# A two-layer transformer decoder: the first layer's inverse roots taken by VectorE from the variance's bits, in place of ScalarE's logarithm and exponential

## The chip, the cores and the metric

The kernel runs on one core of a Trainium2 chip. Its time is the device time of one execution in microseconds (us). The median of three runs before the change is 869.42 us (866.59 to 870.5). The engines are called PE (TensorE), DVE (VectorE), ACT (ScalarE), POOL (GpSimd) and SP (SyncE, which here only issues transfers) in the rows of the profile.

## The reference, cut to what matters

The input `x` is 16 sequences of 128 tokens with 128 numbers each. Layer 0 is self attention, cross attention and a mixture of experts, layer 1 is attention, a cosine block and a quantised MLP. Each step reads the normalised `x` and adds its result to `x`:

```python
def _layernorm(x, axis=-1, eps=1e-05):
    m = jnp.mean(x, axis=axis, keepdims=True)
    v = jnp.var(x, axis=axis, keepdims=True)
    return (x - m) / jnp.sqrt(v + eps)

x = x + _L0_attn_ref(_layernorm(x, axis=-1), ...)    # 16 heads of 8 numbers, causal
x = x + _L0_xattn_ref(_layernorm(x, axis=-1), ctx_768, ...)
x = x + _L0_ffn_ref(_layernorm(x, axis=-1), ...)
```

The change concerns `1 / sqrt(v + eps)` of the first two of these normalisations, 2 x 16 tiles of 128 tokens. The inverse roots are numbers of one per token: 128 partitions x 1 for a tile, and 128 x 4 for the four tiles of a group that are treated together.

## The kernel before, in words

`layer0_attentions` runs both attentions of layer 0 as one pipeline over N = 32 steps: t = 0 to 15 is the self attention of sequence t, t = 16 to 31 the cross attention of sequence t - 16. The loop is unrolled, from t = -4 to 32, and each engine has its own list of instructions in this order; only semaphores tie them together. In iteration t:

- PE computes the scores of step t (`scores`, lines 454 and 458: the second needs a row of maxima that SP's transfer has laid out), transposes the maxima of t + 1 and projects the output of t - 1 (`back_part`), makes queries and keys of t + 3 and transposes the normalised tile of t + 4, in cross attention the context tile `l_cb` too (`front_part`, line 407), multiplies with the floors (line 467, cross attention), computes the raw scores of t + 2 for the row maxima (`maxima`, line 442) and multiplies probabilities with values (`values`, line 485).
- DVE: reciprocal of the sums of t - 1 (`finish`, line 704), a copy (`expand_values`), the normalised output (`weighted`), the normalised tile of t + 4 (`normalise`, while that tile belongs to the first sixteen), the clips in cross attention (line 699), the statistics of the new `x` (line 658), and four reductions for the maxima of t + 2 (`top`, line 684), with `moments` between the first and the second of them and other small work between the second and the third. PE's `scores(t + 1)` waits for all four reductions of `top` (semaphore `maxed`).
- ACT: four exponentials of step t (line 545), copies of PE's results (lines 558 and 525), and the split of the queries for t + 3 (line 539, in cross attention 533 and 536).
- POOL: adds the output bias (line 335), adds the attention's result to `x` (line 358), splits the keys (line 340), and normalises the tiles of the cross attention (line 330).

The inverse roots are made for four tiles at a time. k = 0 is the input's normalisation, group g = 0 to 3 of the sixteen input tiles; k = 1 is the normalisation ahead of cross attention, for the tiles that self attention has finished. DVE adds eps (`variance`). ACT takes the logarithm and then the exponential of -0.5 times it (`roots`, lines 579 and 581; each of the two is preceded by a load of an activation table). DVE improves the result by one Newton step of three instructions (`scales`, lines 649, 651, 653), y(1.5 - 0.5 v y^2).

Their places: `roots(0, 0)` and `scales(0, 0)` ahead of the loop; `roots(0, g)` at the end of t = -2, 2, 6 and `scales(0, g)` at t = -1, 3, 7, behind `normalise` and ahead of the statistics; `variance(1, g)` at t = 4, 8, 12, 16 between the second and the third reduction of `top`; `roots(1, g)` at the end of t = 5, 9, 13, 17; `scales(1, g)` at t = 6, 10, 14, 18 between the second and the third reduction.

Ahead of everything ACT issues nine transfers, the last seven of them the self attention's weights (semaphore `weights`, which PE and DVE wait for as a whole), the last being `self_bo`. At t = 3 SP issues the cross attention's weights, in 22 transfers, and from t = 2 on it writes a blank pattern to memory for the expert stage.

## Time and profile before

| | |
|---|---|
| median of three runs | 869.42 us |
| the profiled execution's own time | 870.21 us |
| its span (first to last instruction) | 867.4 us |
| PE busy | 623.3 us (72%), 6449 matmuls |
| DVE busy | 532.8 us (61%), 1414 instructions |
| ACT busy | 379.7 us (44%), 884 instructions |
| POOL busy | 217.1 us (25%), 312 instructions |
| layer 0's two attentions | from 0 to about 300 us |

The page gives busy time and instructions of each engine, and the groups of instructions that cost most. Busy shares are means over stages with different limits. The attention stage is read best from a timeline, which lists instructions in the order of their start with their duration, and in brackets how long the engine was idle before them and what ended that. "issue" there means that nothing in the profile shows what the engine waited for. Reading one engine's timeline from a line to the same line of the next iteration gives the length of an iteration.

### The profile page before, as it was taken

Reading aid. Unit: us, or ns where it says so; the run is one execution under the profiler, and the core shown is the slowest. Engines: PE = TensorE matmul, PEld = TensorE weight load, DVE = VectorE, ACT = ScalarE, POOL = GpSimd, SP = SyncE. Lnnn points to the kernel's source line nnn. Section 1 sums busy time; section 2 is a strip of 40 time slices with the busy share of each in tenths; the row PEclk is TensorE's granted clock in tenths of the full one; section 3 lists DMA queues with packets and bytes.
Section 4 is the critical chain, followed back from the end, with each engine's and each line's share of the span. In section 5 each row is a group of like instructions: output and inputs, shape, how many; then the busy total and the mean of one; then the engine's idle time right before and its main releaser. Section 6 shows DMA issues by size and latency. Waiting matters only on the chain. (4 is left out here: it accounts for less than half of the span.)

```text
span 867.4 us, 17861 instructions
## 1 busy us (share of the span) xinstructions
PE 623.3 (72%) x6449; PEld 460.8 (53%) x6449; DVE 532.8 (61%) x1414; ACT 379.7 (44%) x884; POOL 217.1 (25%) x312
## 2 busy tenths in 40 slices
PE   3896999889999572056665714989999973875765
PEld 1453555556666362045655602667787852653554
DVE  3463565587788563236564467565665733877995
ACT  6464656777666321033333302543525334543332
POOL 3132223344342116513232214132221310000000
PEclk9798999999999955579999965999999995556797
DMA  3013153341110031155555530000000001000000
GB/s 91 2 43 95 53 127 102 102 104 36 52 27 8 5 140 48 44 195 226 223 212 219 216 98 0 2 2 2 2 2 2 2 1 28 14 1 0 12 13 24
DMA packets 54146, 55.81 MB, mean 64 GB/s; under 512 B 10492, under 2 KB 44862, under 8 KB 54062
## 3 DMA queue, kind: packets, MB, share of 16 engines
q1 hardware_dynamic: 50493, 49.52, 17.7%
q0 software_dynamic: 2272, 4.27, 1.5%
q8 instruction: 51, 0.84, 0.4%
q10 hardware_dynamic: 1296, 0.92, 0.4%
q14 instruction: 34, 0.27, 0.1%
HBM read 16.66 MB, written 14.49 MB: 36 GB/s over the span
## 5 line engine op out<-in xcount | busy, mean ns | idle before, releaser
L545 ACT ACTIVATE l_probs<-bank 128x512 f32<-128x512 f32 x128 | 66.1, 603 | 98.0 <-PE bank L458 97.9
L1073 ACT ACTIVATE experts_h<-bank,experts_wb 128x128 f32<-128x128 f32 x156 | 44.5, 368 | 86.0 <-PE bank L1047 81.7
L1432 POOL COPY ptx<-over_pt 32x512 f32<-32x512 f32 x64 | 38.9, 607 | 128.1 <-DVE over_pt L1402 120.3
L1080 POOL DMA_INDIRECT results<-experts_y,experts_dest x39 | 40.2, 1030 | 99.8 <-DVE experts_y L1115 99.3
L1040 PE MATMUL bank<-ident,experts_xb 128*128 128x128 f32 x39 | 13.2, 338 | 67.4 <-DMA experts_xb<-slots 67.4
L699 DVE SCALAR_TENSOR_TENSOR l_probs<-l_probs,bank 128x512 f32<-128x512 f32 x64 | 41.1, 684 | 24.9 <-PE bank L467 23.1
L684 DVE TENSOR_REDUCE l_m<-bank 128x4 f32<-128x512 f32 x64 | 40.9, 678 | 19.4 <-PE bank L442 19.4
L454 PE MATMUL bank<-l_qxx,l_front 32*128 32x512 f32 x256 | 37.4, 651 | 19.2 <-issue 15.5
L358 POOL TENSOR_TENSOR x<-x,l_back 128x128 f32<-128x128 f32 x32 | 14.5, 454 | 132.5 <-ACT l_back L558 121.4
L1040 PEld LDWEIGHTS bank<-ident,experts_xb 128*128 128x128 f32 x39 | 5.5, 142 | 74.7 <-DMA experts_xb<-slots 74.7
L1332 ACT ACTIVATE ke<-bank 64x512 f32<-64x512 f32 x64 | 37.9, 592 | 16.3 <-PE bank L1263 15.5
L1047 PE MATMUL bank<-experts_xt,experts_wb 128*128 128x128 f32 x312 | 43.1, 283 | 0.0
L658 DVE BATCH_NORM_STATS2 l_stats<-x 128x6 f32<-128x128 f32 x32 | 9.3, 291 | 54.3 <-POOL x L358 54.3
L1055 PE MATMUL bank<-experts_wb,experts_h 128*128 128x128 f32 x312 | 41.3, 275 | 0.3 <-ACT experts_h L1073 0.3
L684 DVE TENSOR_REDUCE l_m_raw<-bank 128x4 f32<-128x512 f32 x64 | 40.7, 673 | 0.0
L1047 PEld LDWEIGHTS bank<-experts_xt,experts_wb 128*128 128x128 f32 x312 | 39.5, 198 | 0.0
L892 POOL DMA_INDIRECT slots<-xs,route_pos x32 | 30.9, 966 | 29.6 <-DVE route_pos L964 20.4
L1055 PEld LDWEIGHTS bank<-experts_wb,experts_h 128*128 128x128 f32 x312 | 38.0, 192 | 0.5 <-ACT experts_h L1073 0.5
L1306 PE MATMUL bank<-over_ot,over_wo 128*128 128x128 f32 x256 | 33.3, 284 | 6.0 <-DVE over_ot L1408 6.0
L1375 DVE COPY over_q<-bank 128x512 f32<-128x512 f32 x32 | 22.1, 690 | 24.7 <-PE bank L1263 24.7
L1099 DVE COPY experts_xt<-bank 128x128 f32<-128x128 f32 x39 | 11.4, 291 | 41.0 <-PE bank L1040 40.9
L340 POOL TENSOR_TENSOR l_kxx<-l_front,heads 128x512 f32<-128x512 f32 x32 | 33.3, 1039 | 11.9 <-ACT l_front L525 10.6
(318 smaller groups left out, 1709.1 us busy)
## 6 DMA issues: line engine op xcount, KB each, us to landing
experts_wb<-w SPq DMA_DIRECT2D x39, 578.0 KB
slots<-blank SPq DMA_DIRECT2D x16, 528.0 KB, 4.7
w<-in_w SPq DMA_DIRECT2D x16, 256.0 KB
experts_xb<-slots SPq DMA_DIRECT2D x39, 66.0 KB, 1.8
experts_both<-results SPq DMA_DIRECT2D x8, 256.0 KB, 5.1
x<-in_x SPq DMA_DIRECT2D x4, 256.0 KB, 3.9
out<-x SPq DMA_DIRECT2D x4, 256.0 KB, 2.3
l_cb<-in_ctx SPq DMA_DIRECT2D x16, 48.0 KB
```

Of the source, the lines that this page charges most:

```text
L340: nc.gpsimd.tensor_tensor(kxx[t % 2][:, :, :], front[(t - 3) % 4][:, 1, :].rearrange("p (a k) -> p a k", a=1).broadcast_to([128, 4, S]), M ...
L454: nc.tensor.matmul(score_bank[g][:, :], k[r, :], qxx[t % 4][r, :, :].rearrange("p j q -> p (j q)"), start=True, stop=False, skip_group_che ...
L545: nc.scalar.activation(probs[t % 2][:, g, :], score_bank[g][:, :], ACT.Exp, scale=SCALE0).then_inc(s["probs"], 1)
L684: nc.vector.tensor_reduce(mx[:, 4 * g:4 * g + 4], top_bank[g][:, :].rearrange("p (j k) -> p j k", j=4), AX.X, ALU.max, negate=True).then_i ...
L699: nc.vector.scalar_tensor_tensor(probs[t % 2][:, g, :], probs[t % 2][:, g, :], 1.0, floor_bank[g][:, :], ALU.min, ALU.max).then_inc(s["cli ...
L1047: mm = nc.tensor.matmul(up_bank[j % 2][:, c * S:(c + 1) * S], wb[j % 4][:, W1 + c * 128:W1 + (c + 1) * 128], xt[j % 2][:, :], start=True, ...
L1055: mm = nc.tensor.matmul(down_bank[j % 2][:, 0:D], h[j % 2][:, c, :], wb[j % 4][:, W2 + c * D:W2 + (c + 1) * D], start=(c == 0), stop=(c == 3))
L1073: nc.scalar.activation(h[j % 2][:, c, :], up_bank[j % 2][:, c * S:(c + 1) * S], ACT.Gelu_apprx_tanh, bias=wb[j % 4][:, B1 + c:B1 + c + 1]) ...
L1080: nc.gpsimd.indirect_dma_start(M.results, bass.IndirectOffsetOnAxis(dest[j % 4][:, 0:1], 0), y[j % 4][:, :], None, bounds_check=2 * B * S ...
L1306: mm = nc.tensor.matmul(y_bank[:, 0:S], wo[:, r, :], ot[t % 2][:, r, :], start=r == 0, stop=r == PAIR - 1)
L1332: nc.scalar.activation(ke[h, r, j, :], ring[at_block(t, r, 1) % 3][h, :], ACT.Copy).then_inc(s["ke"], 1)
L1432: nc.gpsimd.tensor_copy(ptx[t % 2][r, :, r], pt[t % 2][r, :, :]).then_inc(s["spread"], 1)
```

## The change

`roots` and ACT's part in it are gone. DVE makes a first estimate from the variance's bits: it shifts the pattern right by one and subtracts it from the constant 0x5F3759DF, both on 32-bit integers, and then takes three Newton steps of the same three instructions as before. That is SCALE_STEPS = 11 instructions in place of three, each of which waits for the one before it. They are cut in three parts: the estimate and the first Newton step (five instructions), the second step (three), the third (three). For k = 0 the parts stand at t = -3, -2, -1 (group 1), 1, 2, 3 (group 2) and 5, 6, 7 (group 3), at the place where `scales` stood; for k = 1 at t = 4, 5, 6 (group 0), 8, 9, 10, then 12, 13, 14, then 16, 17, 18, between the second and the third reduction. Group 0 of the input is done in one piece ahead of the loop.

```diff
-                def roots(k, g):
-                    r = slice(B * k + 4 * g, B * k + 4 * g + 4)
-                    wait(act, s[f"var{k}"], g, plus=1)
-                    nc.scalar.activation(log[:, r], var[:, r], ACT.Ln).then_inc(s[f"ln{k}"], 1)
-                    wait(act, s[f"ln{k}"], g, plus=1)
-                    nc.scalar.activation(root[:, r], log[:, r], ACT.Exp, scale=-0.5).then_inc(s[f"root{k}"], 1)
...
-                roots(0, 0)
...
-                    if t in (-2, 2, 6):
-                        roots(0, (t + 6) // 4)
-                    if t in (5, 9, 13, 17):
-                        roots(1, (t - 5) // 4)
...
+GUESS, SCALE_STEPS = float(0x5F3759DF), 11
+PARTS = range(0, 5), range(5, 8), range(8, SCALE_STEPS)
...
-                def scales(k, g):
+                def scales(k, g, steps):
...
+                    for n in steps:
+                        if n == 0:
+                            wait(dve, s[f"var{k}"], g, plus=1)
+                            V.tensor_scalar(half[k][:, :], var[:, r].bitcast(I32), 1, None, ALU.logical_shift_right).then_inc(s[f"newton{k}"], 1)
+                            continue
+                        wait(dve, s[f"newton{k}"], g, per=SCALE_STEPS - 1, plus=n)
+                        if n == 1:
+                            V.tensor_scalar(root[:, r].bitcast(I32), half[k][:, :], -1.0, GUESS, ALU.mult, ALU.add).then_inc(s[f"newton{k}"], 1)
+                        elif n % 3 == 2:
+                            V.scalar_tensor_tensor(square[k][:, :], root[:, r], -0.5, root[:, r], ALU.mult, ALU.mult).then_inc(s[f"newton{k}"], 1)
+                        elif n % 3 == 0:
+                            V.tensor_tensor(slope[k][:, :], square[k][:, :], var[:, r], ALU.mult).then_inc(s[f"newton{k}"], 1)
+                        elif n < SCALE_STEPS - 1:
+                            V.scalar_tensor_tensor(root[:, r], slope[k][:, :], 1.5, root[:, r], ALU.add, ALU.mult).then_inc(s[f"newton{k}"], 1)
+                        else:
+                            V.scalar_tensor_tensor(rstd[:, r], slope[k][:, :], 1.5, root[:, r], ALU.add, ALU.mult).then_inc(s[f"ready{k}"], 1)
...
-                scales(0, 0)
+                scales(0, 0, range(SCALE_STEPS))
...
-                    if t in (-1, 3, 7):
-                        scales(0, (t + 5) // 4)
+                    if t in (-3, -2, -1, 1, 2, 3, 5, 6, 7):
+                        scales(0, (t + 7) // 4, PARTS[(t + 3) % 4])
...
-                    if t in (6, 10, 14, 18):
-                        scales(1, (t - 6) // 4)
+                    if 4 <= t < 19 and t % 4 != 3:
+                        scales(1, t // 4 - 1, PARTS[t % 4])
```

At the start, on ACT, this stood between the weights' transfers and the first copy of a front in the program before:

```order
L593 ACT_TABLE_LOAD
L593 ACTIVATE self_identb<-ident 128x128
L579 ACT_TABLE_LOAD
L579 ACTIVATE l_log<-l_var 128x4
L581 ACT_TABLE_LOAD
L581 ACTIVATE l_root<-l_log 128x4
L525 ACTIVATE l_front<-bank 128x128
```

and this stands there after the change (the lines are numbered anew):

```order
L588 ACT_TABLE_LOAD
L588 ACTIVATE self_identb<-ident 128x128
L529 ACTIVATE l_front<-bank 128x128
```

The logarithm and the exponential are gone with their two table loads. In the rest of ACT's attention stage no load is left; the next one is that of the routing's square root.

On DVE, iteration t = 8, this stood between the statistics of the finished tile and the reciprocal of the next iteration in the program before:

```order
L658 BN_STATS l_stats<-x 128x6
L684 TENSOR_REDUCE l_m<-bank 128x4
L663 BN_AGGR l_mv<-l_stats 128x2
L684 TENSOR_REDUCE l_m<-bank 128x4
L642 TENSOR_SCALAR l_var<-l_mv 128x4
L684 TENSOR_REDUCE l_m<-bank 128x4 x2
L704 RECIPROCAL l_rden<-bank 128x128
```

and this after the change:

```order
L659 BN_STATS l_stats<-x 128x6
L685 TENSOR_REDUCE l_m<-bank 128x4
L664 BN_AGGR l_mv<-l_stats 128x2
L685 TENSOR_REDUCE l_m<-bank 128x4
L632 TENSOR_SCALAR l_var<-l_mv 128x4
L642 TENSOR_SCALAR l_half<-l_var 128x4
L646 TENSOR_SCALAR l_root<-l_half 128x4
L648 SCALAR_TENSOR_TENSOR l_square<-l_root 128x4
L650 TENSOR_TENSOR l_slope<-l_square,l_var 128x4
L652 SCALAR_TENSOR_TENSOR l_root<-l_slope,l_root 128x4
L685 TENSOR_REDUCE l_m<-bank 128x4 x2
L705 RECIPROCAL l_rden<-bank 128x128
```

The five instructions of part 0 have come between the variance and the third reduction. At t = 9 nothing stood there before, and part 1 stands there now:

```order
L659 BN_STATS l_stats<-x 128x6
L685 TENSOR_REDUCE l_m<-bank 128x4
L664 BN_AGGR l_mv<-l_stats 128x2
L685 TENSOR_REDUCE l_m<-bank 128x4
L648 SCALAR_TENSOR_TENSOR l_square<-l_root 128x4
L650 TENSOR_TENSOR l_slope<-l_square,l_var 128x4
L652 SCALAR_TENSOR_TENSOR l_root<-l_slope,l_root 128x4
L685 TENSOR_REDUCE l_m<-bank 128x4 x2
L705 RECIPROCAL l_rden<-bank 128x128
```

Here the three reductions behind `moments`, which followed each other, are cut in one and two. At t = 10 the same three names stand in the same place before and after.

## Rows read from the trace of the kernel before

**Rows 1.** The page, part 1: busy us (share) x instructions of TensorE.
```profile
PE 623.3 (72%) x6449; PEld 460.8 (53%) x6449; DVE 532.8 (61%) x1414; ACT 379.7 (44%) x884; POOL 217.1 (25%) x312
```

**Rows 2.** Line 579 alone: count, ns min/median/max, first and last start.
```profile
L579 ACT ACT_TABLE_LOAD  x8: 1283/1283/1283, 7.2 to 184.1; - x8
```

**Rows 3.** Timeline, ScalarE: start, duration, instruction, [idle before it, releaser].
```profile
117.34 1.28 ACT L579 ACT_TABLE_LOAD   x1
...
121.12 2.06 ACT L545 ACTIVATE l_probs<-bank 128x512 f32<-128x512 f32 x4 [0.76 <-PE bank L458]
...
187.03 2.04 ACT L545 ACTIVATE l_probs<-bank 128x512 f32<-128x512 f32 x4
```

**Rows 4.** Timeline, VectorE, iterations t = 9 and 10.
```profile
111.43 0.95 DVE L704 RECIPROCAL l_rden<-bank 128x128 f32<-128x128 f32 x1
...
119.26 0.95 DVE L704 RECIPROCAL l_rden<-bank 128x128 f32<-128x128 f32 x1
...
125.91 0.16 DVE L649 SCALAR_TENSOR_TENSOR l_square<-l_root 128x4 f32<-128x4 f32 x1
126.10 0.16 DVE L651 TENSOR_TENSOR l_slope<-l_square,l_var 128x4 f32<-128x4 f32 x1
...
127.57 0.95 DVE L704 RECIPROCAL l_rden<-bank 128x128 f32<-128x128 f32 x1
```

**Rows 5.** Timeline, TensorE, the scores of t = 10 and 11.
```profile
119.45 1.14 PE L454 MATMUL bank<-l_qxx,l_front 32*128 32x512 f32 x8 [0.43 <-issue]
...
127.75 1.14 PE L454 MATMUL bank<-l_qxx,l_front 32*128 32x512 f32 x8 [0.90 <-issue]
```

**Rows 6.** Timeline, TensorE, the iterations t = 18 and 19.
```profile
184.75 1.14 PE L454 MATMUL bank<-l_qxx,l_front 32*128 32x512 f32 x8 [0.44 <-issue]
...
188.80 0.33 PE L407 MATMUL bank<-ident,l_cb 128*128 128x128 f32 x1 [0.43 <-DMA l_cb<-in_ctx]
...
193.98 1.14 PE L454 MATMUL bank<-l_qxx,l_front 32*128 32x512 f32 x8 [0.98 <-issue]
...
197.43 0.27 PE L407 MATMUL bank<-ident,l_cb 128*128 128x128 f32 x1
```

**Rows 7.** Timeline, start: VectorE, TensorE; then `self_bo`: issue, us to landing.
```profile
10.22 0.16 DVE L649 SCALAR_TENSOR_TENSOR l_square<-l_root 128x4 f32<-128x4 f32 x1 [4.66 <-ACT l_root L581]
11.08 0.22 DVE L161 COPY self_wq<-self_wide_q 128x128 f32<-128x128 f32 x1
14.16 0.29 DVE L675 COPY v_exp<-bank 128x128 f32<-128x128 f32 x1 [0.75 <-PE bank L475]
...
11.31 0.45 PE L404 MATMUL bank<-ident,l_xn 128*128 128x128 f32 x1 [11.31 <-DVE l_xn L668]
...
4.93 0.59 ACTq L151 DMA_DIRECT2D self_bo<-in_self_bo  x1
...
DMA to landing us min/median/max: 5.7/5.7/5.7
```

**Rows 8.** Timeline, VectorE, then GpSimd, at t = 12, 13 and 18.
```profile
142.29 0.42 DVE L642 TENSOR_SCALAR l_var<-l_mv 128x4 f32<-128x4 f32 x1
...
149.97 1.85 DVE L684 TENSOR_REDUCE l_m<-bank 128x4 f32<-128x512 f32 x3
...
192.13 0.15 DVE L649 SCALAR_TENSOR_TENSOR l_square<-l_root 128x4 f32<-128x4 f32 x1
...
142.22 0.46 POOL L335 TENSOR_TENSOR x<-x,cross_bo 128x128 f32<-128x128 f32 x1
...
150.46 0.46 POOL L335 TENSOR_TENSOR x<-x,cross_bo 128x128 f32<-128x128 f32 x1
...
191.97 0.82 POOL L330 TENSOR_SCALAR l_xn<-x,l_mv,l_rstd 128x128 f32<-128x128 f32 x1
```

**Rows 9.** Timeline, VectorE, t = 1.
```profile
43.57 0.29 DVE L658 BATCH_NORM_STATS2 l_stats<-x 128x6 f32<-128x128 f32 x1 [1.67 <-POOL x L358]
```

**Rows 10.** Timeline, TensorE, t = 5.
```profile
79.39 2.07 PE L458 MATMUL bank<-row,self_side 128*128 128x512 f32 x4 [7.89 <-DMA row<-l_back]
```

More of the change, by code:

```diff
@@ L209, in layer0_attentions @@
         s = semaphores(nc, "l0", """x0 x1 x2 x3 consts weights prepared masks heads cleared floors
-            stats0 aggr0 stats1 aggr1 var0 ln0 root0 square0 slope0 ready0 var1 ln1 root1 square1 slope1 ready1 xn cload front_ps front qd qxx kxx v_exp
+            stats0 aggr0 stats1 aggr1 var0 newton0 ready0 var1 newton1 ready1 xn cload front_ps front qd qxx kxx v_exp
             smax_ps maxed m_clip back_ps back mt_hi mt row st_ps probs pv rden o_norm x_done
@@ L231, in layer0_attentions @@
         mv, rstd = sb("mv", [S, N, 2]), sb("rstd", [S, N])
-        var, log, root = sb("var", [S, N]), sb("log", [S, N]), sb("root", [S, N])
+        var, root = sb("var", [S, N]), sb("root", [S, N])
+        half = [sb(f"half{k}", [S, 4], I32) for k in range(2)]
         square, slope = [sb(f"square{k}", [S, 4]) for k in range(2)], [sb(f"slope{k}", [S, 4]) for k in range(2)]
@@ L642, in variance @@
                     nc.vector.tensor_scalar(var[:, r], mv[:, r, 1], EPS_LN, None, ALU.add).then_inc(s[f"var{k}"], 1)
-                def scales(k, g):
+                def scales(k, g, steps):
                     r = slice(B * k + 4 * g, B * k + 4 * g + 4)
-                    wait(dve, s[f"root{k}"], g, plus=1)
-                    nc.vector.scalar_tensor_tensor(square[k][:, :], root[:, r], -0.5, root[:, r], ALU.mult, ALU.mult).then_inc(s[f"square{k}"], 1)
-                    wait(dve, s[f"square{k}"], g, plus=1)
-                    nc.vector.tensor_tensor(slope[k][:, :], square[k][:, :], var[:, r], ALU.mult).then_inc(s[f"slope{k}"], 1)
-                    wait(dve, s[f"slope{k}"], g, plus=1)
-                    nc.vector.scalar_tensor_tensor(rstd[:, r], slope[k][:, :], 1.5, root[:, r], ALU.add, ALU.mult).then_inc(s[f"ready{k}"], 1)
+                    V = nc.vector
+                    for n in steps:
[14 more added lines that the diff above has]
+                            V.scalar_tensor_tensor(rstd[:, r], slope[k][:, :], 1.5, root[:, r], ALU.add, ALU.mult).then_inc(s[f"ready{k}"], 1)
                 def statistics(t):
```

## The prediction, made before the changed kernel was run

> **What bounds the kernel now.** I read the page first: TensorE is busy 72% of the span [rows 1], and the change does not touch it, so the question is which waits of TensorE the touched engines end. I then looked for the stage that the change reaches, which is the first 195 us of 867.4, and read ScalarE, VectorE and TensorE there in order of time.
>
> ScalarE is what the change relieves. It loads an activation table 16 times for eight pairs of logarithm and exponential, 1283 ns each [rows 2]; line 581 has as many loads of the same length as the row of line 579 shows. But most of these pairs stand in idle time. The pair of t = 9 begins at 117.34 and is over before 121.12, and the first exponential of the next iteration still waits 0.76 us for TensorE [rows 3]. Only the pair of t = 17 makes it late: that exponential starts at 187.03, right behind the pair, with no wait in its row [rows 3].
>
> What sets the pace is a loop of two engines: TensorE's maxima feed four reductions on VectorE (`top`), and the next scores (line 454) wait for the last of these. The reader should see it in two numbers that agree. An iteration without small instructions among the reductions takes 119.26 - 111.43 = 7.83 us on VectorE; the one with three of them takes 127.57 - 119.26 = 8.31, which is 0.48 more [rows 4]. And TensorE's idle time before line 454 goes from 0.43 to 0.90 us at the same place, 0.47 more, though the row names "issue" there and not VectorE [rows 5]. So whatever stands between the second and the third reduction is paid in full.
>
> **What the change takes away.** ScalarE loses 16 x 1.283 = 20.5 us of table loads [rows 2] and 16 small activations. By the idle times above nearly nothing of it is on the path. At t = 17 the late exponential is hidden by something else: TensorE's line 407 waits until 188.80 for the transfer of `l_cb`, while in iteration t = 19 it starts 197.43 - 193.98 = 3.45 us after line 454, and here it would have started at 184.75 + 3.45 = 188.20 [rows 6]. This wait of 0.6 us is not ScalarE's, so I count nothing for the relief at t = 17.
>
> At the start VectorE waits 4.66 us for the first root, until 10.22, and three instructions later the first tile is normalised; TensorE begins at 11.31 [rows 7]. Now the eleven instructions start at 10.22 - 4.66 = 5.56 and take 11 x 0.2 = 2.2 us, so rstd is there at 7.8 instead of 10.8. That is 3.0 us, but what is late next is the weights: TensorE waits for all seven transfers, and the last one (`self_bo`) is issued at 4.93 and lands 5.7 us later, at 10.63 [rows 7]. I let TensorE begin at 10.70. Lower bound of the gain: VectorE's copy, which needs the same transfers, starts at 11.08, so they had landed by then, which leaves 0.2 us. Upper bound: 3.0 us, if the landing were early. I take 11.31 - 10.70 = 0.61, the landing's own row. Against it stands the next place: at t = -3 five new instructions come ahead of `expand_values`, where VectorE had 0.75 us idle [rows 7]; 5 x 0.19 = 0.95 us, so 0.20 is paid. The start brings 0.61 - 0.20 = **0.4 us**.
>
> **What the change adds.** The step from one dependent small instruction to the next is 126.10 - 125.91 = 0.19 us [rows 4], and I use it for the new ones, integer ones included (bounds: 0.15, the shortest duration among them, and 0.42, the longest [rows 8]).
>
> For the input's groups (t = -2 to 7) the parts follow `normalise`, and VectorE then waits for GpSimd. The shortest such wait is that of t = 1, behind the statistics of four tiles, 1.67 us [rows 9]; the five new instructions there take 0.95. Nothing of these parts is paid.
>
> For the second normalisation's groups the parts stand between the second and the third reduction, in three iterations of every four. Part 0 (five instructions, behind a variance that stands there already) costs 5 x 0.19 = 0.95; part 1 costs 0.47, as the three instructions do today; part 2 has three instructions where three stood, so nothing. Per place:
> - t = 4: part 0, 0.95. Hidden: TensorE waits 7.89 us for the row's transfer until 79.39 in the next iteration [rows 10], and that transfer is queued behind the cross weights on SP, not behind VectorE.
> - t = 5, 9: part 1, 0.47 each; t = 8, 12, 16: part 0, 0.95 each. Paid.
> - t = 13: part 1, 0.47. Here the second reduction and the two behind it start at 149.97 and take 1.85, so the first new instruction would start at about 150.56, while GpSimd's addition runs from 150.46 to 150.92 [rows 8]. Under the same addition, begun at 142.22, the variance at 142.29 took 0.42 us [rows 8] where such instructions take 0.16; so 0.26 more, 0.73.
> - t = 17: part 1, 0.47. Line 454 moves to 185.22, line 407 could start at 188.67, and `l_cb` lands at 188.80 as before [rows 6]: hidden. SP issues that transfer without asking VectorE.
>
> Sum: 2 x 0.47 + 3 x 0.95 + 0.73 = 4.5 us. All places together cost 4.5 + 0.95 + 0.47 = 5.9 if nothing hides.
>
> The 0.26 at t = 13 agrees with a rule of the Trainium skill, page "SBUF — State Buffer", section "SBUF: two separate sides": a VectorE instruction with two inputs in SBUF and a GpSimd instruction that reads SBUF lock each other out for the whole instruction. By the rule GpSimd's TENSOR_SCALAR (line 330) would lock too, and part 1 of t = 17 would wait some 0.5 us for it, of which the `l_cb` wait hides a little: the sum would be 0.4 us higher. The trace speaks against that: with line 330 running from 191.97 to 192.79, the SCALAR_TENSOR_TENSOR at 192.13 took its usual 0.15 us [rows 8]. I leave it out.
>
> **Sum.** -0.4 + 4.5 = +4.1 us. The profiled execution took 870.21 us around its span of 867.4; 4.1 more gives 874.3. It was 0.8 above the median of the runs, 869.42; from the median the forecast is **873.5 us**, 0.47% slower. What this kernel's measurement can tell from no change is about 0.5%, 4.35 us, so the forecast lies just inside "same".
>
> **Rivals.**
> 1. *No cover (slower).* The places t = 4 and t = 17 are paid as well, and the weights land at 11.0, so the start gives nothing. For it: the row transfer of t = 5 and `l_cb` may come earlier when VectorE's side is later. Against it: 7.89 us is a wide cover. The price is +5.9, 875.3. It decides as soon as one of both places is paid along with a start of under 0.2 us gain. Chance 13%.
> 2. *The integer pair is slow (slower).* The shift and the subtraction, at 0.42 us like the longest row instead of 0.16, cost 2 x 0.26 at each of t = 8, 12, 16: +1.6 on the forecast, 875.1. For it: no integer operation of this size stands in VectorE's rows. Against it: at four elements the kind of number should not matter. Chance 6%.
> 3. *The reductions are not what TensorE waits for (not slower).* If "issue" in the row of line 454 means its own sequencer, and the loop's extra 0.48 us at t = 10 came from elsewhere, the added instructions are free. What is left is the start, -0.4, and perhaps the 0.6 us of t = 17: 868.4 to 869.0. For it: the label. Against it: both views give the same 0.47. Chance 13%.
> 4. *The whole start is saved.* If TensorE can begin at 8.3, the start gives 3.0 - 0.2 = 2.8 us and the change costs 4.5 - 2.8 = +1.7, 871.1. Against it: the landing row. Chance 6%.
> 5. *ScalarE sets the pace (faster).* Then the 20.5 us of loads go from the path and 4.5 come back: 853.4. Against it: the 0.76 us idle behind the pair. Chance 2%.
>
> **How the numbers follow.** The forecast has 60%. Its own range is 871.7 to 875.3: the start between 0.2 and 0.9, each part's step between 0.15 and 0.22, and the scatter of the medians (the three runs before lie 3.9 us apart). The range that should hold the time 8 times in 10 takes in rivals 1, 2 and 4: 870.2 to 876.7. Slower by over 0.5% means above 873.8: 42% of the forecast's 60%, and most of rivals 1 and 2, together 41%. Faster by over 0.5% is rival 5 and a tail of rival 3, 4%. The rest is 55%.
>
> **What would show it.** In the profile after: TensorE's first matmul at about 10.7; no table load on ScalarE between the first one and the routing; VectorE's step from the reciprocal (the old line 704) to the next at t = 8, 12 and 16 longer by 0.95 than the variance alone made it, at t = 5, 9 and 13 by 0.47 to 0.73; line 454's idle time longer by as much; t = 4 and t = 17 without effect on the row's and `l_cb`'s waits, which get shorter instead. The first attention stage would end 4.1 us later, and the stages behind it take the same time as before. The prediction is wrong if line 454 keeps 0.43 us of idle at t = 9, or if the difference stands behind 300 us, where nothing was changed.

## The result, and the profile of the changed kernel

The changed kernel takes 875.55 us (median of six runs, 874.67 to 878.4) against 868.63 (864.99 to 870.5) for the kernel before on the same chip: the ratio is 1.0093, with a 95% interval of 1.0066 to 1.0119. Two later comparisons, described with the experiments, give 1.0057 and 1.007; all three together make the changed kernel 6.1 ± 1.0 us slower. So it is slower, by more than the bound of 0.5%; the forecast of 873.5 us was too low and its "same" wrong, though the time lies inside the range given.

The page's busy times answer to [rows 1]:

```profile
PE 615.1 (70%) x6419; PEld 458.1 (52%) x6449; DVE 543.8 (62%) x1478; ACT 356.2 (41%) x852; POOL 217.9 (25%) x312
```

ScalarE is busy 23.5 us less, VectorE 11.0 us more, and the span is 873.5 us instead of 867.4. The kernel became slower although the sum of busy time fell by more than it rose.

ScalarE's table loads answer to [rows 2]. These are all that the timeline of the changed kernel shows before 320 us (start, duration, instruction, idle time before it and what ended it):

```profile
5.17 1.28 ACT L588 ACT_TABLE_LOAD   x1 [5.17 <-issue]
...
309.88 1.28 ACT L195 ACT_TABLE_LOAD   x1 [2.69 <-PEq L119]
```

VectorE's timeline of the changed kernel, iterations t = 8 and 9, answers to [rows 4]:

```profile
104.38 0.94 DVE L705 RECIPROCAL l_rden<-bank 128x128 f32<-128x128 f32 x1
...
111.00 0.16 DVE L632 TENSOR_SCALAR l_var<-l_mv 128x4 f32<-128x4 f32 x1
111.20 0.17 DVE L642 TENSOR_SCALAR l_half<-l_var 128x4 int32<-128x4 int32 x1
111.40 0.17 DVE L646 TENSOR_SCALAR l_root<-l_half 128x4 int32<-128x4 int32 x1
111.61 0.16 DVE L648 SCALAR_TENSOR_TENSOR l_square<-l_root 128x4 f32<-128x4 f32 x1
111.80 0.16 DVE L650 TENSOR_TENSOR l_slope<-l_square,l_var 128x4 f32<-128x4 f32 x1
112.00 0.16 DVE L652 SCALAR_TENSOR_TENSOR l_root<-l_slope,l_root 128x4 f32<-128x4 f32 x1
...
113.28 0.94 DVE L705 RECIPROCAL l_rden<-bank 128x128 f32<-128x128 f32 x1
...
121.57 0.94 DVE L705 RECIPROCAL l_rden<-bank 128x128 f32<-128x128 f32 x1
```

The five new instructions begin 0.20 us apart, the integer ones too. From reciprocal to reciprocal, t = 8 takes 113.28 - 104.38 = 8.90 us and t = 9 takes 8.29.

TensorE's timeline of the changed kernel shows the scores that come out of it, and answers to [rows 5]:

```profile
104.56 1.14 PE L458 MATMUL bank<-l_qxx,l_front 32*128 32x512 f32 x8 [0.43 <-issue]
...
113.46 1.14 PE L458 MATMUL bank<-l_qxx,l_front 32*128 32x512 f32 x8 [1.51 <-issue]
...
121.75 1.14 PE L458 MATMUL bank<-l_qxx,l_front 32*128 32x512 f32 x8 [0.90 <-issue]
```

The idle time ahead of the scores grows from 0.43 to 1.51 us behind part 0 and to 0.90 behind part 1.

This gives a ruler for the whole stage: the step from one iteration's scores to the next (line 454 before, 458 after), in us. Each kernel of the experiments below was read with it (columns: iteration t; "copy" is a second profile of the kernel before; "1, 2, 3" are three profiles of the changed kernel):

```
 t    before   copy   | changed 1     2      3   | parts_out all_out before_out four_steps
 4      7.90   7.90   |    8.90    8.91   8.91   |   7.90     7.82     7.90       8.91
 5     17.24  19.47   |   16.75   16.62  18.51   |  18.89    18.26    17.31      18.68
 6      8.31   8.29   |    8.30    8.30   8.29   |   7.85     7.83     7.83       8.29
 7      7.81   7.83   |    7.82    7.83   7.82   |   7.82     7.83     7.84       8.30
 8      7.90   7.90   |    8.90    8.92   8.90   |   7.92     7.83     7.92       8.90
 9      7.83   7.82   |    8.29    8.30   8.32   |   7.83     7.82     7.82       8.29
12      8.25   8.25   |    9.33    9.33   9.33   |   8.07     8.01     8.26       9.34
13      7.94   7.94   |    8.65    8.66   8.65   |   7.95     7.95     7.93       8.65
16      9.43  10.04   |   10.41   10.96  10.64   |   9.52     9.66    10.00       9.91
17      8.10   8.10   |    8.60    8.60   8.60   |   8.11     8.12     8.12       8.60
18      9.23   9.37   |    8.78    9.30   9.30   |   9.31     9.13     8.97       8.96
```

Most rows repeat to 0.03 us between profiles of one kernel. Those with a transfer in them (t = 5, 16 and 18) scatter, and so does the first step (t = 0), which is about 9.1 us in some profiles and 10.2 to 10.6 in others. Two single steps outside this table stand out as well: t = 15 of parts_out (8.03 against 7.41) and t = 13 of second_only (10.01 against 8.65); both are taken up below.

At t = 12 and 13 one new instruction each time meets GpSimd's addition, as forecast for t = 13. VectorE's, then GpSimd's timeline of the changed kernel, which answer to [rows 8]:

```profile
144.86 0.41 DVE L642 TENSOR_SCALAR l_half<-l_var 128x4 int32<-128x4 int32 x1
...
153.92 0.40 DVE L648 SCALAR_TENSOR_TENSOR l_square<-l_root 128x4 f32<-128x4 f32 x1
...
188.48 0.16 DVE L648 SCALAR_TENSOR_TENSOR l_square<-l_root 128x4 f32<-128x4 f32 x1
...
144.79 0.45 POOL L339 TENSOR_TENSOR x<-x,cross_bo 128x128 f32<-128x128 f32 x1
...
153.84 0.46 POOL L339 TENSOR_TENSOR x<-x,cross_bo 128x128 f32<-128x128 f32 x1
...
188.37 0.79 POOL L334 TENSOR_SCALAR l_xn<-x,l_mv,l_rstd 128x128 f32<-128x128 f32 x1
```

The two small instructions that begin under line 339's addition take 0.41 and 0.40 us and end when it ends (144.86 + 0.41 = 145.27 against 144.79 + 0.45 = 145.24); the one under line 334's TENSOR_SCALAR takes 0.16. On this the rule of the Trainium skill that the prediction weighed ("SBUF — State Buffer", section "SBUF: two separate sides") and the trace differ again at the same place: by the rule line 334 would have locked too.

At the start, VectorE's, GpSimd's and TensorE's timelines of the changed kernel answer to [rows 7]:

```profile
7.85 0.16 DVE L654 SCALAR_TENSOR_TENSOR l_rstd<-l_slope,l_root 128x4 f32<-128x4 f32 x1
...
10.01 0.23 DVE L164 COPY self_wq<-self_wide_q 128x128 f32<-128x128 f32 x1 [1.62 <-DMA self_bo<-in_self_bo]
...
13.00 1.04 DVE L652 SCALAR_TENSOR_TENSOR l_root<-l_slope,l_root 128x4 f32<-128x4 f32 x1
...
13.97 0.28 DVE L676 COPY v_exp<-bank 128x128 f32<-128x128 f32 x1
...
12.99 1.04 POOL L344 TENSOR_TENSOR l_kxx<-l_front,heads 128x512 f32<-128x512 f32 x1 [1.49 <-ACT l_front L529]
...
10.07 0.45 PE L408 MATMUL bank<-ident,l_xn 128*128 128x128 f32 x1 [10.07 <-DMA self_bo<-in_self_bo]
```

The scales are there at 8.0, as forecast, and the weights are what TensorE then waits for. They landed at 10.01 in place of 10.63, so the first matmul starts at 10.07. But the last instruction of part 0 at t = -3 stands for 1.04 us behind line 344 of GpSimd, and the copy behind it starts at 13.97, only 0.19 us earlier than before.

### The profile page after: what moved, and what is told of

Read it like the earlier page. It is cut to its first block and busy times, and to the rows that moved or that the text cites. A ratio compares the mean times of both kernels' runs of the same rounds, so it can differ in the third digit from the quotient of the medians.

```text
span 873.5 us, 17863 instructions
## 1 busy us (share of the span) xinstructions
PE 615.1 (70%) x6419; PEld 458.1 (52%) x6449; DVE 543.8 (62%) x1478; ACT 356.2 (41%) x852; POOL 217.9 (25%) x312
## 5 line engine op out<-in xcount | busy, mean ns | idle before, releaser
L1048 PEld LDWEIGHTS bank<-experts_xt,experts_wb 128*128 128x128 f32 x312 | 39.3, 198 | 0.0
L489 PE MATMUL bank<-l_probs,v_exp 128*32 128x128 f32 x1024 | 35.5, 280 | 2.6 <-DVE l_probs L700 2.6
```

The lines of the kernel that those rows point to most:

```text
L489: mm = nc.tensor.matmul(pv_bank[32 * g:32 * g + 32, part * S:(part + 1) * S], w, probs[t % 2][:, g, j * S:(j + 1) * S], start=(j == 0), st ...
L1048: mm = nc.tensor.matmul(up_bank[j % 2][:, c * S:(c + 1) * S], wb[j % 4][:, W1 + c * 128:W1 + (c + 1) * 128], xt[j % 2][:, :], start=True, ...
```

## The experiments

The kernels were timed in three groups, each on one chip with the kernel before among them; each ratio is to that kernel on the same chip, and ± stands for 95% on a difference of means. The kernel before had a median of 868.84 us in the first group, 871.01 in the second (the dose and the early loads) and 867.86 in the third (again2, before_copy, all_out, before_out).

**The change in halves.** input_only has the first normalisation's groups (k = 0) by bits and Newton steps and the second's (k = 1) by logarithm and exponential; second_only is the other way round. In short, for input_only:

```diff
-    if t in (-2, 2, 6):
-        roots(0, (t + 6) // 4)
...
+    if t in (-3, -2, -1, 1, 2, 3, 5, 6, 7):
+        newton(0, (t + 7) // 4, PARTS[(t + 3) % 4])
```

> Only the input's normalisation (k = 0) takes its roots from the variance's bits; the second normalisation keeps ScalarE's logarithm and exponential and the three instructions at t = 6, 10, 14, 18. Theory A: the scores of t = 1 start 0.3 us later than in the kernel before (39.3) although TensorE's first matmul is 1.2 us earlier, the last scores near 290.7, in all 868.5 to 870. Rival (the start gives what it was forecast to, -0.4, and the changed kernel's start was scatter): scores of t = 1 at 38.6 or earlier.

Measured: 868.04 against 868.84, ratio 0.9986 (0.9971 to 1.0). The time is just under the range of theory A, and the scores of t = 1 start at 38.03, which is what the rival named (38.6 or earlier: the start gives the 0.4 us that it was forecast to) and not the 39.3 of theory A. Other profiles with the new start have them between 37.84 and 39.29, so this one does not settle it.

> Only the second normalisation (k = 1) takes its roots from the variance's bits, with the parts among the reductions; the input keeps logarithm and exponential. Theory A: the start as in the kernel before (scores of t = 1 at 39.0), the last scores 4.9 us later than before, near 295.3, in all 873 to 876. Rival (the two halves of the change cost alike): 871 to 872.

Measured: 872.28, ratio 1.0048 (1.0028 to 1.0067), between the two theories. The loss is in the second half, and the first half brings at most a little: input_only is 0.9 ± 1.0 us below the kernel before, second_only 3.8 ± 1.5 above it. The ruler shows the same: second_only has 8.91, 8.90 and 8.29 at t = 4, 8 and 9, input_only has 7.90, 7.89 and 7.83. In second_only t = 13 took 10.01: there TensorE's granted clock was 0.50 from 150 to 152 us, and the four matmuls of its line 461 lasted 1.84 us where the changed kernel's lasted 1.21. No other profile has this, so the ends of the stage in two profiles should be compared step by step and not as one number.

**The parts out of the reductions.** parts_out computes the same, but the three parts of a second group stand behind `normalise`, one iteration later, where VectorE waits for GpSimd:

```diff
+    if 5 <= t < 20 and t % 4 != 0:
+        scales(1, (t - 5) // 4, PARTS[(t - 5) % 4])
...
-    if 4 <= t < 19 and t % 4 != 3:
-        scales(1, t // 4 - 1, PARTS[t % 4])
```

> The changed kernel with the second normalisation's Newton parts moved one iteration later, behind the normalised tile and ahead of the statistics (t = 5, 6, 7 and so on), so that nothing but moments and the variance stands among the reductions. Theory A: the last scores start 7 us earlier than in the changed kernel, near 288.6 (295.60, less four parts 0 of 0.98 of which that of t = 4 was hidden, less parts 1 at t = 5, 9, 13 with 0.5 to 0.7, less four parts 2 of 0.47), 867 to 869 us in all, at or below the kernel before. Rival (the reductions are not what TensorE waits for, something else in the stage got slower): 873 us or more.

Measured: 867.55, ratio 0.9982 (0.9964 to 1.0); the changed kernel without this edit (again) was at 873.74 on the same chip. With the same instructions, 6.2 us are gone (6.3 ± 1.9 by the means). The ruler shows every added term gone (t = 4, 8, 9, 13, 17), and 0.47 less than the kernel before at t = 6 (and at t = 10 and 14), where the three old instructions had stood. So it is the place that costs. What comes back is `l_cb`: beside the wait for it at t = 16, which all profiles but that of four_steps have, TensorE's timeline of parts_out has one at t = 15, which makes that step 8.03 in place of 7.41, and one at t = 18. In the changed kernel's three profiles the first of these is missing and the second is at most 0.21.

```profile
163.49 0.33 PE L411 MATMUL bank<-ident,l_cb 128*128 128x128 f32 x1 [0.75 <-DMA l_cb<-in_ctx]
...
189.85 0.33 PE L411 MATMUL bank<-ident,l_cb 128*128 128x128 f32 x1 [0.99 <-DMA l_cb<-in_ctx]
```

**Everything out, and the old way out.** all_out moves the variance as well; before_out is the kernel before with its `scales(1, ...)` moved to the same idle place, tables and all. This pair asks what the new arithmetic is worth when both stand well. The edit of before_out:

```diff
+    if t in (7, 11, 15, 19):
+        scales(1, (t - 7) // 4)
...
-    if t in (6, 10, 14, 18):
-        scales(1, (t - 6) // 4)
```

> The changed kernel with all of the second normalisation's small instructions, the variance too, behind the normalised tile (t = 5, 6, 7 and so on), the cross weights where they were. Theory A: 7 to 8 us under the changed kernel less what `l_cb` takes back at t = 13 to 18, so 866 to 868, 0.1 to 0.4% under the kernel before. Rival (as parts_out, the waits for transfers take everything back): 868.5 or more.

Measured: 866.45 against 867.86, ratio 0.9983 (0.9969 to 0.9998).

> The kernel before with its own three instructions moved out of the reductions, to t = 7, 11, 15, 19 behind the normalised tile; ScalarE's logarithm and exponential stay. It asks what the roots on VectorE are worth once the place is right. Theory A (the place is everything, ScalarE's table loads stand in idle time): the iterations of t = 6, 10, 14, 18 each 0.47 us shorter, 866 to 868, the same as all_out within 0.15%. Rival (taking the table loads from ScalarE brings something by itself): all_out is faster than this one by 0.3% or more.

Measured: 866.37, ratio 0.9982 (0.9966 to 0.9999). Both are 1.4 to 1.5 us below the kernel before by their medians, roughly what four places of 0.47 us make, less a wait for `l_cb`. Between them the difference of means is 0.2 ± 1.4 us, where the rival wanted 0.3% (2.6 us) or more. So sixteen table loads less are worth nothing that these runs resolve: they stood in idle time. VectorE's timeline of all_out shows the idle place with two parts in it (t = 6), and what it leaves:

```profile
88.69 0.17 DVE L648 SCALAR_TENSOR_TENSOR l_square<-l_root 128x4 f32<-128x4 f32 x1
...
91.97 0.29 DVE L659 BATCH_NORM_STATS2 l_stats<-x 128x6 f32<-128x128 f32 x1 [2.10 <-POOL x L362]
```

Even behind six small instructions VectorE waits 2.10 us there for GpSimd.

**A dose.** four_steps adds a fourth Newton step to every group. The second groups get it as a part of their own at t = 7, 11, 15 and 19 among the reductions; the input's groups get theirs inside their last part, in the idle place. (The expectation is wrong on the input's groups: all of them have the fourth step, not only the first.)

```diff
-GUESS, SCALE_STEPS = float(0x5F3759DF), 11
-PARTS = range(0, 5), range(5, 8), range(8, SCALE_STEPS)
+GUESS, SCALE_STEPS = float(0x5F3759DF), 14
+PARTS = range(0, 5), range(5, 8), range(8, 11), range(11, SCALE_STEPS)
+PARTS0 = range(0, 5), range(5, 8), range(8, SCALE_STEPS)
...
-                        scales(0, (t + 7) // 4, PARTS[(t + 3) % 4])
+                        scales(0, (t + 7) // 4, PARTS0[(t + 3) % 4])
...
-    if 4 <= t < 19 and t % 4 != 3:
+    if 4 <= t < 20:
```

> The changed kernel with a fourth Newton step for the second normalisation, three more instructions among the reductions at t = 7, 11, 15 and 19 (the input's first group gets four steps too, ahead of the loop; its other groups keep three... and end with the third). Theory A: the iterations of t = 7, 11, 15, 19 are each 0.47 us longer, except where `l_cb` is waited for; 1.4 to 1.9 us more than the changed kernel, 875 to 876. Rival (the reductions are not what TensorE waits for): no change from 873.7.

Measured: 878.96 against 871.01, ratio 1.0102 (1.0074 to 1.0129). The ruler has t = 7 at 8.30 (before and changed 7.82), t = 11 at 8.75 (7.98), t = 15 at 8.40 (7.41) and t = 19 at 8.59 (8.12), while t = 16, with its transfer, gave 0.5 to 1.1 back. Over the kernel before it is 8.9 ± 2.1 us slower, that is 2.8 ± 2.3 more than the changed kernel's 6.1; the expectation had 1.4 to 1.9 more, and nothing for the rival. VectorE's, then GpSimd's timeline of four_steps at t = 7, 11 and 15:

```profile
104.52 0.15 DVE L649 SCALAR_TENSOR_TENSOR l_square<-l_root 128x4 f32<-128x4 f32 x1
...
138.31 0.45 DVE L649 SCALAR_TENSOR_TENSOR l_square<-l_root 128x4 f32<-128x4 f32 x1
...
172.53 0.64 DVE L649 SCALAR_TENSOR_TENSOR l_square<-l_root 128x4 f32<-128x4 f32 x1
...
138.28 0.46 POOL L340 TENSOR_TENSOR x<-x,cross_bo 128x128 f32<-128x128 f32 x1
...
172.11 1.04 POOL L345 TENSOR_TENSOR l_kxx<-l_front,heads 128x512 f32<-128x512 f32 x1
```

The three instructions cost 0.47 us at t = 7 and 19, and 0.77 and 0.99 at t = 11 and 15. The rows show what is added: at t = 11 the first of them begins under GpSimd's addition (line 340) and takes 0.45 us in place of 0.15, at t = 15 under the product on 512 elements (line 345) and takes 0.64. Both end within 0.02 us of GpSimd's instruction. So the cost of a place is its 0.47 us and the time by which such a meeting stretches an instruction, here 0.30 and 0.49.

**The cover of t = 4.** Here the cross weights are loaded at t = -1 and no longer at t = 3, so that the row's transfer of t = 5 has nothing ahead of it. If the row's wait is what hid part 0 of t = 4, the changed kernel must now lose more against its like.

```diff
-    if t == 3:
+    if t == -1:
         M.cross_weights.load(sp, d, s["cross_weights"])
```

> The kernel before, with SP issuing the cross attention's weights at t = -1 in place of t = 3, so that the row's transfer of t = 5 does not stand behind them. Only a base for the next two. Both theories: the wait of 7.9 us before line 458 at t = 5 goes, with the slow clock behind it; 859 to 862 us, if the 22 issues at t = -1 delay no row.

Measured: 865.88 against 871.01, ratio 0.994 (0.9916 to 0.9963). That is above the 859 to 862 expected, whose condition (no row delayed by the issues at t = -1) did not hold: the step of t = 5 falls from 17.24 us to 7.83, and that of t = 1, where the load now stands, rises from 7.82 to 15.19.

> The changed kernel with the same edit. Theory A (each part among the reductions costs its instructions times 0.19 us wherever no transfer is waited for, and t = 4 was hidden by the row's transfer alone): the iteration of t = 4 is 1.0 us longer as before, and now it counts, so this kernel is 5 to 6.5 us slower than before_early, 865 to 867. Rival (t = 4 was free for another reason, the change costs what the median says): 4 to 5 us slower than before_early. Start, theory A (what TensorE gains at its first matmul is lost again in the slow stretch of its clock): scores of t = 1 within 0.5 us of those of before_early. Rival: 0.4 to 1 us earlier.

Measured: 869.09, ratio 0.9983 (0.9961 to 1.0005): 3.2 us above before_early (3.6 ± 2.2 by the means), less than either theory had. The place itself is as forecast: without the row's wait, t = 4 takes 8.92 against 7.91 us and t = 5 takes 8.29 against 7.83, and both stay in the sum. But the load brings a wait at t = 1 instead, and there the changed kernel is the quicker one. SP's queue and TensorE in before_early:

```profile
23.65 0.65 SPq L279 DMA_DIRECT2D row<-l_back  x1
...
43.71 2.07 PE L458 MATMUL bank<-row,self_side 128*128 128x512 f32 x4 [4.76 <-DMA row<-l_back]
```

and in after_early:

```profile
21.99 0.65 SPq L283 DMA_DIRECT2D row<-l_back  x1
...
41.76 1.44 PE L462 MATMUL bank<-row,self_side 128*128 128x512 f32 x4 [2.64 <-DMA row<-l_back]
```

The first row's transfer is issued 1.66 us earlier and the step of t = 1 is 12.17 us against 15.19. That ScalarE has no table loads ahead of that row any more is my reading of the difference; no run isolates it. With it the two traces add up: t = 1 gives -3.02, t = 4, 5, 8, 9, 12, 13, 16 and 17 give 1.01 + 0.46 + 1.03 + 0.47 + 1.09 + 0.71 + 1.19 + 0.48 = 6.44, t = 18 gives -0.09, and the rest cancels: from the scores of t = 1 to those of t = 31 the difference is 253.15 - 249.82 = 3.33.

all_out_early has both: everything out of the reductions and the early load.

> The changed kernel with the cross weights at t = -1, and with all of the second normalisation's small instructions (the variance and the three parts) behind the normalised tile, at t = 5, 6, 7 and so on: among the reductions only moments is left. Theory A: every iteration up to t = 12 takes 7.8 us, four times (0.47 + 0.07) less than in before_early, 2.2 us, of which the waits for `l_cb` at t = 13 to 18 take back up to 1: 857.5 to 859.5 us, the fastest yet. Rival (VectorE's work ahead of the clips and the statistics costs as much there): as before_early or slower.

Measured: 860.12 (five runs), ratio 0.9882 (0.9854 to 0.9909), just above the range expected. It beats both kernels, by 1.2% the one before. Against before_early, which also has the early load, its trace is 4.5 us shorter from the scores of t = 1 to those of t = 31, but 3.0 of this is the step of t = 1 (12.21 against 15.19), as in after_early; what the places bring is the other 1.5.

**Repeats.** again and again2 are the changed kernel, and before_copy the kernel before, not edited; they show how far one comparison can be trusted.

> The changed kernel once more, nothing edited. Theory A (the parts among the reductions cost about 4.9 us, the start costs 0.3 instead of giving 0.4, and what is left over, some 2 us, is a slow stretch of TensorE's clock at the end of the attention stage that depends on when the stage ends): 873 to 877 us, and the last product with the values (line 489, 32 matmuls a part) takes 1.9 us again, as it did at 301.34, because the stage ends at the same time. Theory B (the 2 us are scatter of a single profiled execution): the same median, but the last product takes 1.08 us this time.

Measured: 873.74 against 868.84, ratio 1.0057 (1.0038 to 1.0077).

> The changed kernel a third time, nothing edited, to tell the size: the first comparison gave 8.1 us over the kernel before, the second 4.9. Theory A (the iterations' excess, 1.0 at t = 8, 12 and 16 and 0.5 to 0.7 at t = 5, 9, 13, with a start worth nothing, 4.9 us): 0.4 to 0.7% over the kernel before, and in the trace t = 8, 9, 12, 13 within 0.1 us of 8.90, 8.30, 9.33, 8.65. Theory B (something behind the attention stage adds 3 us more): 0.8 to 1.0%, and the time from the first table load of the routing to the end 2 to 3 us longer than in before_copy.

Measured: 874.11 against 867.86, ratio 1.007 (1.0047 to 1.0092).

> The kernel before as a kernel of its own, for a second trace of it on the same chip. The same median as the kernel before, within 0.2%. Its trace shows how much the places that depend on a transfer or on TensorE's clock move by themselves: the scores of t = 1 between 37.8 and 39.3, the iteration of t = 5 between 16.6 and 19.0, that of t = 16 between 9.4 and 11.0, while t = 8 stays at 7.90 and t = 9 at 7.83.

Measured: 867.14, ratio 0.9998 (0.998 to 1.0015); t = 5 took 19.47 where 16.6 to 19.0 had been expected, the other places lay in their ranges. The difference of means in the three comparisons of the changed kernel is 8.0 ± 2.0, 5.1 ± 1.5 and 6.1 ± 1.7 us, weighted 6.1 ± 1.0.

again also tested a story of mine. In the first profile TensorE's last value product of the attention is long, at the end where the stage hands over to the routing. The changed kernel's first profile:

```profile
301.34 1.94 PE L489 MATMUL bank<-l_probs,v_exp 128*32 128x128 f32 x32 [1.46 <-DVE l_probs L700]
```

and the same kernel in again:

```profile
301.52 1.08 PE L489 MATMUL bank<-l_probs,v_exp 128*32 128x128 f32 x32 [1.46 <-DVE l_probs L700]
```

I had taken the 0.86 us, and as much in the product behind it, for an effect of the change. The same program at the same time of its stage does it in 1.08, so it differs between executions. That does not clear the change of it: again2 has the two products at 1.54 and 2.00, parts_out and all_out have them long too, and none of the six profiles in which ScalarE still makes logarithms does. With so few profiles I leave it open.

## Why the prediction was wrong, and what of it was right

The mechanism was right, and the verdict was not. What failed is the sum of +4.1 us, and in it first the step "t = 17: hidden", which put a part at nothing: the part costs 0.50 us there, and the wait for `l_cb` gives only about 0.1 of it back on the mean. The parts 0 at t = 8, 12 and 16 were sized some 0.2 us too small in all, and the start's gain of 0.4 is 0.2 ± 0.5 in the traces. The runs showed about +5 by the traces and 6.1 ± 1.0 by the clock in place of +4.1; about 1 us of this has no place. The forecast lay so near the bound of 0.5% that the first of these was enough. By its steps, with "measured" from the ruler:

```
step                            forecast    measured (changed - before)
first matmul                     10.70       10.07
start, up to scores of t = 1     -0.4        -0.2 ± 0.5 (38.60 old start, 38.44 new)
t = 4, part 0                     hidden      +1.00, then hidden
t = 5, part 1                    +0.47       not readable (16.6 to 19.5)
t = 8, part 0                    +0.95       +1.00
t = 9, part 1                    +0.47       +0.47
t = 12, part 0                   +0.95       +1.08
t = 13, part 1 beside GpSimd     +0.73       +0.71
t = 16, part 0                   +0.95       +1.0 (mean of five profiles 10.77, of eight 9.74)
t = 17, part 1                    hidden      +0.50, about 0.1 given back at t = 18
part 2, t = 6, 10, 14             0           0
input's groups                    0           0
sum                              +4.1        about +5; timed +6.1 ± 1.0
```

**Right.** What sets the pace is the loop from the reductions to the next scores, although the row of line 458 says "issue" (rival 3, that the reductions are not what TensorE waits for, is refuted by the ruler, by parts_out and by four_steps). A dependent small instruction costs 0.19 to 0.20 us there. The integer pair lasts 0.17 us each, which refutes the rival of slow integers. The table loads stood in idle time: all_out and before_out are equal within 1.4 us, which refutes the rival that ScalarE sets the pace. The input's parts are free in the loop: input_only is not slower. The collision at t = 13 came with the size that the row of t = 12 gave. The whole start was not saved; the weights were late next, as the text said. The measured 875.55 lies beside the 875.3 of rival 1, but that is luck: it priced both t = 4 and t = 17 as paid and the weights as landing at 11.0, and only t = 17 was (mostly) paid, t = 4 was hidden, and the weights landed earlier than forecast. By its own sign, one of the two places paid and a start worth under 0.2, the rival may still have come true; the start's 0.2 ± 0.5 does not tell.

The row's wait of t = 5 did hide part 0 of t = 4. TensorE's timeline of the changed kernel, which answers to [rows 10]:

```profile
79.81 2.08 PE L462 MATMUL bank<-row,self_side 128*128 128x512 f32 x4 [6.98 <-DMA row<-l_back]
```

The wait is 0.91 us shorter and the row lands at 79.81 against 79.39 before (80.46 in before_copy, 78.98 in again): it moves with the execution, not with VectorE. after_early shows the other side: without this wait the 1.0 us is paid.

**Not decided, the start.** The forecast was 0.61 - 0.20 = 0.4. The first matmul did better: 10.10 on the mean of the nine profiles with the new start against 11.12 on that of the five with the old one. Of this 1.0 us little is left by the scores of t = 1, 38.44 against 38.60, where single profiles scatter by 0.5; so neither 0.4 nor nothing is excluded. Two things are seen on the way. The last instruction of part 0 at t = -3 stands behind line 344 for the 1.04 us of that instruction in every profile with the new start, so that the copy of `v_exp` begins 0.19 earlier in the first profile, and not 1.24. On TensorE this costs 0.25, near the 0.20 forecast: its third transposition of a tile (line 404 before, 408 after) begins 0.8 earlier on the mean and not 1.0. Then TensorE's eight matmuls of the first maxima take longer, 1.79 against 1.42 on the mean, and end only 0.4 earlier. The first row is from the kernel before, the second from the changed one:

```profile
17.66 1.14 PE L442 MATMUL bank<-l_kxx,l_front 32*128 32x512 f32 x8
...
16.67 1.78 PE L446 MATMUL bank<-l_kxx,l_front 32*128 32x512 f32 x8
```

What follows happens under a granted clock that falls to the lower of its two levels for stretches, here from the kernel before (columns: us, then busy time and count of TensorE, its weight loads, VectorE, ScalarE and GpSimd; granted clock; DMA share; GB/s),

```profile
24.00:26.00 2.00, 2.00 (x12) 0.58 (x10) 0.11 (x1) 1.67 (x6) 1.04 (x1) 0.87 0.02 4
...
30.00:32.00 2.00, 2.00 (x8) 1.17 (x5) 0.00 (x0) 0.57 (x2) 0.00 (x0) 0.50 0.00 0
```

and from the changed kernel:

```profile
24.00:26.00 2.00, 2.00 (x11) 0.81 (x10) 0.00 (x0) 0.45 (x2) 0.25 (x1) 0.79 0.00 0
...
30.00:32.00 2.00, 2.00 (x10) 0.99 (x4) 0.00 (x0) 0.29 (x1) 0.00 (x0) 0.50 0.00 0
```

From 30 to 32 us both have a granted clock of 0.50, that is 1.2 of 2.4 GHz, with TensorE busy throughout; their other profiles (before_copy, again, again2) have the same there. Around 24 us the eight matmuls of line 442 (446 after) last 1.14 us in the kernel before and 1.41 in the changed one. That work which begins earlier runs longer at the lower level, and that this takes the rest of the gain, is a reading of these traces; no run isolates it. again2 speaks against it as the only cause: its granted clock was 1.00 from 22 to 26 us, and its scores of t = 0 begin at 28.31, 0.21 before those of the kernel before.

**Wrong, t = 17.** The relief from `l_cb` was put at the full 0.47. TensorE's timeline of the changed kernel answers to [rows 6]:

```profile
185.20 0.27 PE L411 MATMUL bank<-ident,l_cb 128*128 128x128 f32 x1
...
190.33 1.14 PE L458 MATMUL bank<-l_qxx,l_front 32*128 32x512 f32 x8 [0.94 <-issue]
193.91 0.33 PE L411 MATMUL bank<-ident,l_cb 128*128 128x128 f32 x1
```

The wait for `l_cb` at t = 18 (0.43 in the kernel before) is gone in this profile, and 0.21 is left of it in again. But the step of t = 18 gives back 0.45 in the first profile and nothing in the two others (9.30 in both, against 9.23 and 9.37 before). VectorE's and GpSimd's rows show a second cause. They are, in turn, from the first profile and from again:

```profile
197.65 0.16 DVE L654 SCALAR_TENSOR_TENSOR l_rstd<-l_slope,l_root 128x4 f32<-128x4 f32 x1
...
197.54 0.45 DVE L654 SCALAR_TENSOR_TENSOR l_rstd<-l_slope,l_root 128x4 f32<-128x4 f32 x1
...
197.51 0.46 POOL L339 TENSOR_TENSOR x<-x,cross_bo 128x128 f32<-128x128 f32 x1
```

In again the last instruction of part 2 begins 0.03 us into GpSimd's addition and takes 0.45 us; in again2 and after_early the same instruction takes 0.35 and 0.44 under the same addition. In the first profile, and in second_only, it is over before the addition begins. So what the transfer gives back, the collision takes in three profiles of five. Over these five, which have the parts among the reductions, t = 18 takes 9.09 us, and 9.20 over the eight profiles without part 1 at t = 17 (four_steps, with its extra part at t = 15, is left out of both means, here and at t = 16). So some 0.1 of the 0.50 is hidden on the mean, and not all of it.

**Wrong, small.** Part 0 costs 1.00 and not 0.95, since its steps are 0.20 and not 0.19. At t = 12 the collision with GpSimd, which the variance had before, has passed to the shift, so it is not paid twice; 1.08 is the 1.00 and 0.08 more.

**Open.** From the scores of t = 6 to those of t = 16, where nothing scatters, the three profiles of the changed kernel take 82.88, 82.90 and 82.89 us against 79.62, so 3.26 where the forecast had 3.10. With the other places the terms sum to about 5 us, and the runs give 6.1 ± 1.0. What lies between may be at the places that scatter between executions of one program (t = 0, 5, 16, 18 and the end of the attention) or in the error of the timing; I cannot assign it. Behind the scores of t = 31 the span goes on for 577.0 us in the kernel before and 573.8 in its copy, and for 577.9, 574.1 and 576.7 in the changed one: the later stages take the same time within their own scatter, as forecast.

## What to carry to other kernels

Price a small instruction by who waits at its place, not by how busy its engine is: the same three instructions cost 0.47 us between two reductions, 0.8 to 1.0 where they also met a GpSimd instruction, and nothing behind the normalised tile of the next iteration, where VectorE waits for GpSimd anyway. Before moving work off an engine, ask whether its present place is idle: here 16 table loads of 1.28 us were free, and what replaced them was not. Gains that lie ahead of a transfer or of a stretch at the lower clock should be entered with zero among their bounds, and a sum of 4.1 us whose terms are uncertain by 1 us gives no verdict at a bound of 4.35.

## What the runs showed of the hardware that was not expected

- A VectorE instruction on 4 elements per partition lasts 0.15 to 0.17 us. When it begins under one of GpSimd's TENSOR_TENSOR instructions it ends together with that, within 0.04 us in 126 of 133 cases in the fourteen profiles; the other seven began in its last 0.1 us and took their usual 0.15. That makes 0.30 to 0.45 us under the ones on 128 elements, and up to 1.04 (13.00) under the one on 512. Beside GpSimd's TENSOR_SCALAR of 0.79 us no such instruction took more than 0.27 in any of the profiles, and nearly all took 0.15 to 0.18.
- The collision finds a single-input int32 TENSOR_SCALAR too (0.41 us at 144.86).
- Whether it happens can differ between executions of one program: the last instruction of part 2 at t = 18 took 0.16 us in the first profile of the changed kernel and 0.45 in again.
- Integer shift and multiply-add on int32, written to an int32 view of a float tile, took 0.17 us each where float ones took 0.15 to 0.17.
- After a wait of 7 to 9 us for a transfer, the next iteration of TensorE differs by up to 1.7 us between profiles: from the row's landing to the scores of t = 6 it took 8.21 and 9.29 us in the two profiles of the kernel before, and 8.63, 8.55 and 9.90 in the three of the changed one.
